# Twelve subtractions at the end of an attention and expert kernel move from VectorE to GpSimd

## The reference

```python
x = x + attn(_layernorm(x), ...)
# ffn on _layernorm(x), with 8 experts of width 176, two of them for each token
g = silu(einsum('td,edh->teh', x, w_gate)) * einsum('td,edh->teh', x, w_up)
routed = einsum('teh,ehd,te->td', g, w_down, comb)
shared = silu(x @ sw_gate) * (x @ sw_up) @ sw_down      # width 352
out = x_before + routed + shared
```

## Time and profile before

| | us |
|---|---|
| median of 3 runs | 620.45 |
| lowest and highest | 617.01, 621.27 |
| the profiled execution | 623.06 |
| its span, first to last instruction | 621.3 |

### The profile page before, as it was taken

The page is one execution under the profiler, slowest core; times in us unless marked ns, Lnnn a source line. Parts: engine busy times, 40 slices in busy tenths (PEclk is TensorE's granted clock), DMA queues, the critical chain, the costliest instruction groups (busy, mean ns, idle before and its releaser), DMA issues. The chain is left out here.

```text
span 621.3 us, 15625 instructions
## 1 busy us (share of the span) xinstructions
PE 595.6 (96%) x4852; PEld 580.6 (93%) x4852; DVE 490.8 (79%) x1422; ACT 474.5 (76%) x1331; POOL 411.4 (66%) x455
## 2 busy tenths in 40 slices
PE   8998999999999899899999999999989889999995
PEld 8888999999999899899999999999988889999994
DVE  6667886897897989789788987978777866666486
ACT  4778999898998889889898998988966445565531
POOL 1477797696888889878888997988812314444400
PEclk9998999999999999999999999999999989999998
DMA  9792000000001000100100000020412274444292
GB/s 254 237 348 52 2 1 2 3 1 35 11 10 43 11 18 10 44 10 11 43 10 19 23 32 18 3 78 18 145 44 78 94 220 133 127 121 129 78 310 97
DMA packets 34024, 45.41 MB, mean 73 GB/s; under 512 B 4056, under 2 KB 29112, under 8 KB 33944
## 3 DMA queue, kind: packets, MB, share of 16 engines
q1 hardware_dynamic: 29160, 34.56, 17.9%
q0 software_dynamic: 3408, 9.34, 4.6%
q10 hardware_dynamic: 1376, 0.50, 0.3%
HBM read 27.57 MB, written 16.82 MB: 71 GB/s over the span
## 5 line engine op out<-in xcount | busy, mean ns | idle before, releaser
L1260 ACT ACTIVATE probs<-ps_s,nmax 128x256 f32<-128x256 f32 x256 | 119.1, 476 | 23.9 <-DVE nmax L1455 23.0
L233 PE MATMUL ps_q<-xa,wq_hi 128*128 128x256 f32 x512 | 99.5, 292 | 6.9 <-DVE qf L1450 6.8
L1803 POOL TENSOR_TENSOR qswap<-qswap,qsin 128x512 f32<-128x512 f32 x64 | 83.3, 1301 | 32.1 <-ACT qswap L1237 31.9
L1806 POOL TENSOR_TENSOR qf<-qf,qswap 128x512 f32<-128x512 f32 x64 | 82.8, 1294 | 12.7 <-DVE qf L1450 8.5
L1455 DVE TENSOR_REDUCE nmax<-ps_s 128x2 f32<-128x512 f32 x128 | 86.4, 675 | 4.5 <-PE ps_s L233 4.0
L233 PEld LDWEIGHTS ps_q<-xa,wq_hi 128*128 128x128 f32 x512 | 79.0, 191 | 8.7 <-DVE qf L1450 6.6
L1810 POOL TENSOR_TENSOR q_lo<-qf,q_hi 128x512 fp32r<-128x512 f32 x64 | 82.7, 1292 | 5.3 <-ACT q_hi L1237 5.3
L1237 ACT ACTIVATE pT_hi<-ps_t 128x512 fp32r<-128x512 f32 x128 | 76.6, 598 | 11.0 <-PE ps_t L990 9.1
L309 DVE TENSOR_TENSOR pT_lo<-ps_t,pT_hi 128x512 fp32r<-128x512 f32 x128 | 81.9, 681 | 1.5 <-ACT pT_hi L1237 1.5
L233 PE MATMUL ps_s<-kT_hi,q_hi 128*128 128x256 f32 x256 | 77.8, 304 | 1.2 <-ACT probs L1260 1.2
L233 PE MATMUL ps_o<-pT_hi,kv_hi 128*128 128x256 f32 x256 | 76.9, 300 | 1.3 <-ACT norm L1237 1.3
(11 more groups left out here) (330 smaller groups left out, 1879.8 us busy)
## 6 DMA issues: line engine op xcount, KB each, us to landing
xg<-routed_in SPq DMA_DIRECT2D x39, 129.0 KB, 2.3
normal_turned<-xf SPq DMA_DIRECT2D x8, 512.0 KB, 3.0
wq_raw<-Wq_dram SPq DMA_DIRECT2D x16, 192.0 KB, 4.8
x<-x_dram SPq DMA_DIRECT2D x8, 256.0 KB, 5.2
xa<-normal_turned SPq DMA_DIRECT2D x4, 512.0 KB, 4.9
mgu_hi<-routed_out SPq DMA_DIRECT2D x4, 512.0 KB, 6.3
mgu_lo<-routed_out SPq DMA_DIRECT2D x4, 512.0 KB, 9.6
out_dram<-x SPq DMA_DIRECT2D x8, 256.0 KB, 3.6
```

Of the source, the lines that this page charges most:

```text
L233: last = nc.tensor.matmul(out, stat, mov, start=start and n == 0, stop=stop and n == len(terms) - 1, skip_group_check=skip)
L1260: last = nc.scalar.activation(probs[h % 3][:, j, :], L.ps_s[h % 2][:, j, :], ACT.Exp, bias=nmax[:, h % NH, j:j + 1], accum_out=rsum[:, h % ...
L1803: gp.tensor_tensor(qs, qs, L.qsin[:, :].unsqueeze(1).to_broadcast([P, 2, S]), ALU.mult).then_inc(ev.qrot_part, 1)
L1806: gp.tensor_tensor(to, to, qs, ALU.add).then_inc(ev.qrot_done, 1)
```

## The change

VectorE's loop in the tail no longer writes the low parts of units 12 to 23. GpSimd writes them, in a loop of its own behind the 39 `rows_home`, with the same waits and the same semaphore at the end. The low parts of units 0 to 11 stay on VectorE.

```diff
@@ VectorE's loop @@
                     units(*divmod(n, ES))
                 if n in finished:
                     finish(finished[n], 0)
-                if n < ES * B:
-                    unit_lo(*divmod(n, ES))
                 if n in finished:
                     finish(finished[n], 1)
                 if n % ES == 0 and n > ES * FIRST:
@@ GpSimd @@
+            def unit_lo(b, m):
+                n = ES * b + m
+                rows = chunk_rows(m)
+                pool.wait_ge(ev.uhi_done, n + 1)
+                pool.wait_ge(ev.down_done, n - 2)
+                gp.tensor_tensor(u_lo[n % 3][0:rows, :], unit[n % 2][0:rows, :], u_hi[n % 3][0:rows, :].bitcast(F32), ALU.subtract
+                                 ).then_inc(ev.ulo_done, 1)
...
             for j in range(TILES):
                 rows_home(j)
+            for n in range(ES * FIRST, ES * B):
+                unit_lo(*divmod(n, ES))
```

## The result

The changed kernel takes 622.08 us in the median of 22 runs (618.9 to 623.57), the kernel before, run beside it, 620.12 us (22 runs, 616.73 to 622.64). The ratio is 1.003, with a 95% interval of 1.0017 to 1.0044: slower by 1.1 to 2.7 us. That lies within the range that was predicted and within 1%, but it is clear of noise, and more than three times the +0.55 us of the sum.

A forecast was written before the change was run, and what follows sets the result against it. VectorE was taken to set the pace behind 594.45 us. Saving 2.72 us, adding back 2.96 and 0.31, gave +0.55 us on the 620.45 median: 621.0 us, range 617.3 to 623.8.

The forecast's parts named there:

- the sum: Change in total time from all terms: -2.72 + 2.96 + 0.31 = +0.55 us.
- VectorE sets the pace behind the gathers: From 594.45 to 616.34 us VectorE is busy 21.10 of 21.89 us and bounds the kernel there.
- one `u_lo` costs 0.34 us: VectorE's time per low-part subtraction in the tail; taking away those of units 15 to 22 saves 2.72 us.
- The first three: Subtractions of units 12 to 14, moved to GpSimd behind its last scatter: claimed to cost nothing.
- The holding: Units 15 to 22: GpSimd's subtraction delays finish's third multiply-add on VectorE by 0.37 us each, 2.96 us in all.
- The twelfth: Unit 23's subtraction, on the chain that ends last: slower on GpSimd, 0.74 instead of 0.42 to 0.43, +0.31 us.
- the likeliest case of the forecast: The forecast as reckoned: near +0.55 us, median 621.0 us, own range 619.5 to 622.5, chance 0.55.
- The faster rival: VectorE's multiply-adds in finish aren't held, or GpSimd enters harmlessly: -2.4 us, 618.0 us; chance 0.2.
- The clock's gift of 0.6 us: Last down on TensorE: if its clock stayed up, some 0.6 us more gained, 617.4 us; part of the faster rival.
- The slower rival: GpSimd reads one instruction sooner, delaying finish's second multiply-add by 0.71 us: +3.3 us, 623.7; chance 0.2, whole instructions lost included.
- The Trainium skill's rule: VectorE with two SBUF inputs and GpSimd fully block each other for whole instructions: 0.71 us late each time, +3.3 us.

The follow-up runs named there:

- e5: Kernel before, plus a GpSimd drain right behind the 39 scatters and a tiny memset at GpSimd's end waiting for the last low part: 620.13 us against 620.69.
- e9: Changed kernel, with low parts of units 12 to 14 back on VectorE and a GpSimd drain behind its scatters: 619.63 us against 619.96 for the kernel before.
- e10: Kernel before, units 15 to 21 on GpSimd after its own drain, started behind finish's third multiply-add; last finish behind unit 23's low part: 618.37 us against 621.11.
- e11: As e10, but without GpSimd's wait for the third multiply-add: 620.37 us against 621.11 for the kernel before, ratio 1.0012.
- e3: Kernel before, plus a tiny memset at GpSimd's end waiting for the last accumulate: 624.04 us against 619.96.
- e4: Changed kernel, with GpSimd's twelve subtractions replaced by memsets that only write zeros: 619.58 us against 620.69 for the kernel before.
- e8: Kernel before, with the last finish (batch 6) moved behind unit 23's low part, run twice: ratios 0.9976 and 0.9984.

## Why the prediction was right or wrong

The time came out at 622.08 us, the prediction was 621.0, and its range held. Point by point:

- *VectorE sets the pace behind the gathers; one `u_lo` costs 0.34 us.* Right. With nothing held (the writes-only kernel) unit 23 starts 2.6 us earlier than before; 2.72 was the sum.
- *The first three cost nothing.* Right: GpSimd's take 0.73 to 0.74 us there, and unit 15 starts 4.80 us behind unit 12 in both kernels. (The matmul at 590.73 reads the high part, not the low one; what holds is that `down` waits for the low part ahead of its first matmul.)
- *The holding, 0.37 us a time.* Right, to the instruction, for seven of the eight: the third multiply-add takes 0.83 to 0.85 instead of 0.48, GpSimd's subtraction 0.84 to 0.86. At unit 15 it was the first, 0.58 us longer; from that `unit` to the next it is 3.81 us instead of 3.68. The two runs that take the reads away and double them moved the time both ways as worked out.
- *The twelfth, +0.31 us.* Right: 0.72 instead of 0.42.
- *The sum, +0.55 us.* Right up to the last `accumulate`, where the traces give +0.61, and in the kernel with the drain moved, whose tail is 0.6 longer.
- *What failed* is a term that the sum doesn't have. I put GpSimd's place in the program's end at nothing: "Nothing stands behind it on GpSimd but the other eleven". Something did, the drain with which GpSimd ends. It was hidden before and shows up in no view of waits or chain of that kernel. It takes 5.87 us behind the last instruction, as it already did in the trace of before (588.72 to 594.59), and adds 1.2 us. 0.6 and 1.2 are 1.8 us, and 1.96 were measured (1.1 to 2.7). So the range held by its width: the likeliest case of the forecast was short by 1.4 us, most of it this term.
- *The faster rival* fell: multiply-adds with a scalar per partition are held like any other with two SBUF inputs. The clock's gift of 0.6 us isn't tied to it (last section). *The slower rival*, GpSimd reading one instruction sooner, was real at unit 15 alone, and smaller there than its 0.71 us.
- *The Trainium skill's rule* ("SBUF — State Buffer", section "SBUF: two separate sides") was right in kind, and the section "Who interferes with whom" there adds that a GpSimd instruction that only writes doesn't contend, which the writes-only kernel bears out (0.486 us at most). Read as a whole instruction's loss each time it would have given +3.3 us; up to the last `accumulate` +0.6 were lost. Nor did the earlier start decide: at unit 15 of the changed kernel VectorE started 0.05 us ahead of GpSimd and was the one held.

## What to carry to other kernels

In this kernel, work moved from VectorE to GpSimd was free only beside VectorE instructions with at most one SBUF input: each subtraction gave VectorE 0.34 us and took 0.37 back through the wait for its second input. Where it can be started so that it reads beside other instructions, the same move pays (a period of 2.03 to 2.20 instead of 2.37 us). And an engine's end belongs into the sum: look at each engine's drain in the trace of before, and if GpSimd gets work near the program's end, try a drain of its own while it is idle, as here behind the scatters.

## What the runs showed of the hardware that I had not expected

- GpSimd's first drain behind its 71 indirect DMAs ended 5.87 to 5.89 us behind its last instruction in all thirteen kernels, whether it was the drain at the program's end (nine kernels) or one of its own behind the scatters (e5, e9, e10, e11), and whether the instruction ahead of it was a scatter, a subtraction or a memset. The 28 us between the last scatter and this drain in the changed kernel, and the 29 us of idleness in e3, took nothing off. A second drain took 0.17 us behind a memset, and 0.83 to 0.96 us behind a subtraction, most of that the subtraction itself.
- The clock at the end differs from one execution to the next for the same stream. The last `down` took 1.66 us in the kernel before, behind a wait of 0.98 us, and 1.03 us in the kernel with the drain of its own, whose streams on TensorE and VectorE are the same, behind a wait of 1.06 us. The granted clock had fallen from 1.00 to 0.50 (2.4 to 1.2 GHz) at 615.08 in the first, 1.3 us ahead of the last `down`, while TensorE ran the one before it; in the second it fell at 612.28, 0.8 us into the last `down`. That is worth 0.6 us of the tail, which the comparison of two single traces must allow for: in the table it is in the ends of e3, e4 and e5. In both e8 traces and e10 the last `down` was short too (0.97 to 1.06 us), but there the last `accumulate` comes right behind VectorE's own multiply-adds and has no wait for TensorE, so it counts for 0.1 us or so. The chain that ended last of the kernel with its own drain, at the wait for the last low part and the last `down`:

```profile
611.02 0.43 DVE u_lo L309
611.45 0.04 issue
611.50 1.03 PE ps_t L233 x6
```
